# Two-layer block with 16 routed experts on one core: the last batch's scatter, the second half's plan and its pads move among the routed tiles, with eight result buffers

## The chip, the core and the metric

The kernel runs on one core of a Trainium2 chip. The core has TensorE (PE: matmuls and transposes), VectorE (DVE), ScalarE (ACT) and GpSimd (POOL); SyncE (SP) only issues transfers. Transfers with addresses that are computed on the chip (indirect DMAs) are issued by POOL here, all others by SP. The metric is the device time of one execution, in microseconds.

## The reference

Input are 32 sequences of 512 tokens with 256 features, in float32. First comes an attention layer with 16 heads in 4 groups, causal and with rotary positions, between two layer norms and with a residual. Then comes a layer of experts, and the cut below is this one. The kernel computes only the two experts of each token that the router chose.

```python
def _L0_ffn_ref(x, gate_w, gate_b, shared_wg, shared_wu, shared_wd, experts_wg, experts_wu, experts_wd):
    E, TOP_K = 16, 2
    router_logits = jax.nn.sigmoid(x @ gate_w + gate_b)
    expert_values, expert_indices = jax.lax.top_k(router_logits, k=TOP_K)
    expert_values = expert_values / jnp.sum(expert_values, axis=-1, keepdims=True)
    ...
    expert_weighted = jnp.sum(expert_values[..., None] * selected, axis=2)
    return x + _mlp(x, shared_wg, shared_wu, shared_wd) + expert_weighted
x = x + _layernorm(_L0_attn_ref(_layernorm(x)))
x = x + _layernorm(_L0_ffn_ref(_layernorm(x)))
```

(`selected` are the outputs silu(x wg) * (x wu) times wd, 128 wide inside, of the chosen experts.)

## The kernel before

There are two programs for each engine, one after the other, in two blocks, and every engine waits for every other between them.

**The first block** (`attention_phase`) takes the 32 batches through attention, the norms and the router, several batches at once in an order written out by hand. For each batch b DVE ends with the slots (L1094): the place of each token in the list of each of its two experts. POOL then writes the batch's 512 rows to those places in `sorted_dram`, in eight indirect DMAs (`scatter`, L658: four groups of 128 tokens, two experts each), which wait for `slots_ready` and for the copy of the rows, `h2_copied`. The batches are in two halves of 16, each with lists of its own. After the last batch of a half DVE plans its tiles: 28 small steps in three lumps, `plan_ends`, `plan_tiles` and `plan_limits` (L1104 to L1148), which turn the counts of the experts into a table: for each tile its expert, its first row and the limit behind which its rows are padding. SP stores this table (`plan_dram`, L527, elements of 4 bytes, 3 KB in all). Each expert's last tile is filled up with 128 rows of padding, one indirect DMA (a pad) for each of the 16 experts: those of the first half are issued inside attention, and those of the second, whose lists get the last rows only at the very end, inside the second block.

**The boundary** (L330) is a barrier: each engine drains, which includes the transfers that POOL has issued, and then they go on together.

**The second block** (`expert_phases`) begins with SP loading both plans (L1297, L1298) and then the rows of the tiles. Each half has at most 143 tiles of 128 rows, and 286 tiles are run in a fixed order. In turn t:

- SP loads the 128 rows of tile t into one of `RD` = 8 buffers (L1313), as soon as the result of tile t - 8 is taken (`y_taken`, `named`).
- PE transposes the hidden values of tile t - 2 (L1448), the rows of tile t + 1 (L1428), multiplies the rows of tile t by the gate and up weights (L1440, signals `hidden`) and the hidden values of t - 2 by the down weights (L1454).
- ACT copies the transposed hidden values of t - 2 (L1537), takes the silu of tile t (L1531, one instruction to a tile) and halves the rows of t - 2 (L1543).
- DVE copies the transposed rows of t + 1 (L1593), multiplies gate and up of tile t (L1600), works out where the results of t - 2 go (L1609, L1612) and forms the results (L1621) in one of `YD` = 4 buffers. Both of the latter wait until the store of the tile that used the buffer before has landed (`y_stored`).
- POOL waits for `named` and `y_taken`, does one tiny instruction on a cell (L199) and issues the indirect store of the results (L1367). Up to tile 15 it issues one pad of the second half behind it (L1372).

At turn 1, DVE also turns the limits of both halves into two tables, `keep` and `aside` (L1632, L1635, L1639, over 512 columns). When the loads of tile 143 on are issued, SP waits for all scatters and pads of the second half. After the tiles comes the shared expert with the last norm, over 32 batches, to the end.

## Time and profile before

| | us |
|---|---|
| median of three runs | 2648.06 (2647.75 to 2649.0) |
| profiled execution, its time | 2651.59 |
| profiled execution, its span | 2649.8 |
| attention, to the last matmul before the boundary | about 1878 |
| boundary: PE without work | 30.71, up to 1909.17 |
| routed tiles | 1909 to about 2440 |
| shared expert and last norm | 2440 to 2650 |

Over the span PE is busy for 2402.8 us (91%), DVE for 1980.9 (75%), ACT for 1503.2 (57%) and POOL for 1636.4 (62%). The mean granted clock of TensorE is 0.964 of full speed, and it is lower in three places, the start, the boundary and the first tiles. These shares are means over stages with different limits, and so the rows further down are taken from the boundary and the tiles alone. The span runs from the first instruction to the last; the execution's time is 1.8 us more.

### The profile page before, as it was taken

The page shows a single profiled execution, that of the slowest core. Times are in us where ns is not written, and L with a number is a line of the kernel's source. Part 1 is how long each engine was busy: PE and PEld are TensorE (multiplying, and loading weights), DVE is VectorE, ACT ScalarE, POOL GpSimd, SP SyncE. Part 2 cuts the span into 40 slices and gives each one's busy share as a digit, 9 for nine tenths or more (in the row PEclk, how much of TensorE's full clock was granted, in tenths as well). Part 3 has the DMA queues.
Part 4 walks back from the last instruction along what each step waited for, and adds up shares of the span by engine and source line. Part 5 has one row for each costly group of instructions (what it writes and reads, how often), then busy time and mean ns, then how long its engine had stood idle before and what let it go on. Part 6 is the DMA issues. An engine that isn't in the chain of part 4 may idle for free. (4 is left out here: it accounts for less than half of the span.)

```text
span 2649.8 us, 60700 instructions
## 1 busy us (share of the span) xinstructions
PE 2402.8 (91%) x18798; PEld 1582.8 (60%) x18798; DVE 1980.9 (75%) x5220; ACT 1503.2 (57%) x3420; POOL 1636.4 (62%) x2761
## 2 busy tenths in 40 slices
PE   4999999999999999898999999998279999999997
PEld 2565556655566555555655566554168777877664
DVE  5677878778787788677778787874347777776887
ACT  1566666666666666565566666665124444444554
POOL 2446665666656666665666656653266666666886
PEclk7899999999999999999999999999579999999998
DMA  4354445544455443444434444332346546544996
GB/s 124 93 151 123 136 127 153 151 123 135 128 153 151 122 135 121 121 143 144 138 118 123 121 146 146 110 103 74 65 139 190 151 147 200 159 145 156 304 349 237
DMA packets 288652, 388.00 MB, mean 146 GB/s; under 512 B 27922, under 2 KB 238098, under 8 KB 288212
## 3 DMA queue, kind: packets, MB, share of 16 engines
q1 hardware_dynamic: 260788, 308.56, 39.6%
q0 software_dynamic: 27552, 75.57, 8.3%
q8 instruction: 161, 2.64, 0.4%
q14 instruction: 151, 1.24, 0.2%
HBM read 193.40 MB, written 172.27 MB: 138 GB/s over the span
## 5 line engine op out<-in xcount | busy, mean ns | idle before, releaser
L847 ACT ACTIVATE probs<-ps_a 128x512 f32<-128x512 f32 (+1 forms) x1408 | 727.8, 561 | 463.3 <-PE ps_a L731 386.6
L967 DVE TENSOR_REDUCE negmax<-ps_d 128x2 f32<-128x768 f32 (+3 forms) x768 | 788.3, 1040 | 264.2 <-PE ps_d L715 219.8
L713 PE MATMUL ps_d<-ks,qs 96*128 96x128 bf16 (+3 forms) x2048 | 489.2, 305 | 83.5 <-DVE negmax L967 61.7
L729 PE MATMUL ps_a<-qs,ks 99*128 99x512 bf16 (+3 forms) x2048 | 515.0, 305 | 22.3 <-DMA qs<-k_parts_negmax_t 10.2
L731 PE MATMUL ps_a<-mask_exp,ident_bf 128*128 128x128 bf16 x2048 | 396.9, 221 | 0.0
L715 PE MATMUL ps_d<-mask_max,ident_bf 128*128 128x128 bf16 x2048 | 394.9, 222 | 0.0
L1367 POOL DMA_INDIRECT y_dram<-ysb,to_row x286 | 282.3, 987 | 118.5 <-issue 82.3
L713 PEld LDWEIGHTS ps_d<-ks,qs 96*128 96x128 bf16 x2048 | 202.7, 99 | 239.9 <-issue 80.2
L743 PE MATMUL ps_out<-probs,va 128*32 128x512 f32 (+3 forms) x4096 | 333.6, 444 | 0.0
L199 POOL TENSOR_TENSOR pool_cell<-zero_col 1x1 f32<-1x1 f32 x318 | 58.7, 185 | 437.0 <-DVE slot L1094 375.1
L729 PEld LDWEIGHTS ps_a<-qs,ks 99*128 99x128 bf16 x2048 | 201.1, 99 | 187.7 <-issue 39.3
L1440 PE MATMUL ps_gu<-wgu,rows_t 128*128 x1144 | 303.5, 389 | 6.7 <-DVE rows_t L1593 5.3
L658 POOL DMA_INDIRECT sorted_dram<-h,slot x256 | 255.1, 997 | 66.0 <-issue 65.2
L1531 ACT ACTIVATE gate<-ps_gu 128x128 f32<-128x128 f32 x286 | 79.6, 278 | 266.3 <-issue 137.6
L731 PEld LDWEIGHTS ps_a<-mask_exp,ident_bf 128*128 128x128 bf16 x2048 | 203.1, 99 | 29.1 <-issue 19.9
L1440 PEld LDWEIGHTS ps_gu<-wgu,rows_t 128*128 128x128 f32 x1144 | 200.5, 196 | 25.4 <-issue 9.0
L1454 PE MATMUL ps_y<-wd,hid_t 128*128 x572 | 182.7, 402 | 23.4 <-ACT hid_t L1537 22.9
L715 PEld LDWEIGHTS ps_d<-mask_max,ident_bf 128*128 128x128 bf16 x2048 | 203.0, 99 | 0.7 <-issue 0.7
L743 PEld LDWEIGHTS ps_out<-probs,va 128*32 128x32 f32 x4096 | 108.2, 110 | 141.8 <-issue 105.0
L1600 DVE TENSOR_TENSOR hid<-ps_gu,gate 128x128 f32<-128x128 f32 x286 | 83.3, 291 | 120.2 <-ACT gate L1531 96.4
L1593 DVE COPY rows_t<-ps_t 128x256 f32<-128x256 f32 x286 | 118.9, 416 | 35.6 <-PE ps_t L1428 35.1
L1621 DVE SCALAR_TENSOR_TENSOR ysb<-ps_y,rows,half_row 128x256 f32<-128x256 f32 x286 | 138.4, 484 | 9.1 <-PE ps_y L1454 4.2
(200 smaller groups left out, 4516.7 us busy)
## 6 DMA issues: line engine op xcount, KB each, us to landing
qs<-q_stack_dram SPq DMA_DIRECT2D x128, 384.0 KB, 5.8
rows<-sorted_dram SPq DMA_DIRECT2D x286, 129.0 KB
y_in<-y_dram SPq DMA_DIRECT2D x32, 1024.0 KB
q_stack_dram<-q_parts SPq DMA_DIRECT2D x64, 384.0 KB
x_in<-in_x SPq DMA_DIRECT2D x32, 512.0 KB
q_stack_dram<-q_parts SPq DMA_DIRECT2D x64, 256.0 KB
x<-in_x SPq DMA_DIRECT2D x32, 512.0 KB
h_dram<-h SPq DMA_DIRECT2D x32, 512.0 KB, 3.0
```

The lines of the kernel that those rows point to most:

```text
L658: pool.indirect_dma_start(out=sorted_dram[b // (B // 2)][:, :], in_=h2[:, k, j, :], in_offset=None, out_offset=bass.IndirectOffsetOnAxis(a ...
L713: pe.matmul(ps_d[:, number % 2, at:at + width], qs[0:KR, b % 2, h, j * P:(j + 1) * P], ks[0:KR, b % 2, g, 0:width], start=True, stop=False)
L715: ins = pe.matmul(ps_d[:, number % 2, at + j * P:at + (j + 1) * P], ident_bf[:, :], mask_max[:, :], start=False, stop=True)
L729: pe.matmul(ps_a[:, number % 3, at:at + width], ks[0:KM, b % 2, g, j * P:(j + 1) * P], qs[0:KM, b % 2, g * HG + h0 + k, j * P:T], start=Tr ...
L731: ins = pe.matmul(ps_a[:, number % 3, at:at + P], ident_bf[:, :], mask_exp[:, :], start=False, stop=True)
L743: ins = pe.matmul(ps_out[32 * h:32 * h + 32, j * P:T], va[:, b % 3, j, g * 32:(g + 1) * 32], probs[:, at:at + width], start=(j == 0), stop ...
L847: act.activation(probs[:, at:at + nh * width], ps_a[:, number % 3, 0:nh * width], ACT.Exp) \
L967: dve.tensor_reduce(negmax[:, g // 2, j, at:at + nh], src, AX_X, ALU.max, negate=True) \
L1367: pool.indirect_dma_start(out=y_dram[:, :], in_=ysb[:, k, :], in_offset=None, out_offset=bass.IndirectOffsetOnAxis(ap=to_row[k][:, 0:1].bi ...
L1440: ins = pe.matmul(ps_gu[:, t % 2, 0:2 * I], rows_t[:, t % 2, c, :], wgu[:, expert[t], c, :], start=(c == 0), stop=(c == NC - 1))
L1454: pe.matmul(ps_y[:, t % 2, 0:D], hid_t[:, t % 2, :], wd[:, expert[t], :], start=True, stop=True) \
L1621: dve.scalar_tensor_tensor(out=ysb[:, k, :], in0=ps_y[:, t % 2, 0:D], scalar=rows[:, t % RD, D + 1:D + 2], in1=half_row[:, t % 2, :], op0= ...
```

## The change

It has four parts, all around the boundary.

1. The eight scatters of the last batch (b = 31) are no longer issued in the first block. POOL issues them in the second, one behind the result store of each of the tiles 1, 4, 7, ... 22 (`scatter_last`).
2. The plan of the second half leaves the first block as well. DVE does its lumps behind tiles 30, 36 and 42 (`PLAN_AT` = 30); SP stores the table behind the load of tile 46 and loads it back behind that of tile 54. At the start SP loads the first half's plan alone. `keep` and `aside` are formed for each half by itself, at turns 1 and 70.
3. The 16 pads of the second half, issued behind tiles 0 to 15 before, are issued behind tiles 54, 57, ... 99 (`PADS_AT` = 54).
4. There are eight buffers of tile results (`YD` = 8) in place of four.

The buffers that both blocks now use are declared outside of both, and the planning steps stand in a class, `Plan`; the steps themselves are as before. New waits: DVE waits for `plan_stored` before the second plan and for `limits_loaded` at turn 70; SP for `planned` behind tile 46, `plan_stored` behind tile 54, and `plan_loaded` behind tile 142; PE for `plan_loaded` at tile 143.

```diff
-RD, YD = 8, 4
+RD, YD = 8, 8
...
-                if c == B // 2 + 1 or c == B + 1:
-                    half = c // B
-                    sp.wait_ge(planned, half + 1)
-                    sp.dma_start(plan_dram[half].rearrange("w (q p) -> p w q", p=P), tile_plan_i[:, :, :],
+                if c == B // 2 + 1:
+                    sp.wait_ge(planned, 1)
+                    sp.dma_start(plan_dram[0].rearrange("w (q p) -> p w q", p=P), tile_plan_i[:, :, :],
...
-                    if exists(c - 2):
+                    if exists(c - 2) and c - 2 < B - 1:
...
-                        if c - 2 in (B // 2 - 1, B - 1):
+                        if c - 2 == B // 2 - 1:
                             if at == SIDE["plan_ends"]:
-                                plan_ends((c - 2) // (B // 2))
+                                plan.ends(0)
...
+            def load_plan(half):
+                sp.wait_ge(v["plan_stored"], 16 * (half + 1))
+                sp.dma_start(plan_row[:, half, :, :], plan_dram[half, 0:2, :].unsqueeze(0)).then_inc(plan_loaded, 16)
+                sp.dma_start(limits[:, half, :], plan_dram[half, 2, :].bitcast(F32).partition_broadcast(P)) \
+                    .then_inc(limits_loaded, 16)
+
+            load_plan(0)
...
                 load_rows(t)
+                if t == PLAN_AT + 16:
+                    sp.wait_ge(v["planned"], 2)
+                    sp.dma_start(plan_dram[1].rearrange("w (q p) -> p w q", p=P), v["tile_plan_i"][:, :, :],
+                                 allow_slow_non_contiguous=True) \
+                        .then_inc(v["plan_stored"], 16)
+                if t == PLAN_AT + 24:
+                    load_plan(1)
+                if t == TILES - 1:
+                    sp.wait_ge(plan_loaded, 16 * 2)
...
+            def scatter_last(i):
+                if i == 0:
+                    pool.wait_ge(v["slots_ready"], B)
+                    pool.wait_ge(v["h2_copied"], 16 * B)
+                j, k = i // 2, i % 2
+                pool.indirect_dma_start(
+                    out=sorted_dram[1][:, :], in_=v["h2"][:, k, j, :], in_offset=None,
+                    out_offset=bass.IndirectOffsetOnAxis(ap=v["slot"][(B - 1) % 2][:, j, k:k + 1], axis=0),
+                ).then_inc(v["scattered"][(B - 1) % 2], 16)
+
+            def pad_last(e):
+                if e == 0:
+                    pool.wait_ge(v["planned"], 2)
+                pool.indirect_dma_start(
+                    out=sorted_dram[1][:, :], in_=v["pad_row"], in_offset=None,
+                    out_offset=bass.IndirectOffsetOnAxis(ap=v["pad_at"][:, 1, e:e + 1], axis=0),
+                ).then_inc(v["padded"], 16)
...
-                if t < E:
-                    pool.indirect_dma_start(
-                        out=sorted_dram[1][:, :], in_=v["pad_row"], in_offset=None,
-                        out_offset=bass.IndirectOffsetOnAxis(ap=v["pad_at"][:, 1, t:t + 1], axis=0),
-                    ).then_inc(v["padded"], 16)
+                if t % 3 == 1 and t // 3 < 2 * NT:
+                    scatter_last(t // 3)
+                if t >= PADS_AT and (t - PADS_AT) % 3 == 0 and (t - PADS_AT) // 3 < E:
+                    pad_last((t - PADS_AT) // 3)
...
                 if t == 1:
-                    dve.wait_ge(limits_loaded, 16)
...
+                    pads_aside(0)
+                if t == PLAN_AT:
+                    plan.ends(1)
+                if t == PLAN_AT + 6:
+                    plan.tiles(1)
+                if t == PLAN_AT + 12:
+                    plan.limits(1)
+                if t == PLAN_AT + 40:
+                    pads_aside(1)
```

In the programs of the engines it shows at these places. In the rows, `x8` is a run of eight alike, and what stands in brackets are the semaphores waited for.

POOL at the boundary and behind it, before (L658 are the scatters of batch 31, L330 is the boundary, L1353 the start of the second block):

```order
L641 TENSOR_SCALAR shift<-guess 128x4 [waits root_steps]
L199 TENSOR_TENSOR pool_cell<-zero_col 1x1 [waits h2_copied,paused,slots_ready,ln_ready2]
L658 DMA sorted_dram<-h,slot 133248x258 x8
L330 UNCONDITIONAL_BRANCH
L1353 UNCONDITIONAL_BRANCH [waits barrier_Pool_Activation_PE_DVE_SP_gather]
L1356 IOTA own_row 128x512
```

All eight scatters stand here ahead of the boundary, and they leave this place. POOL at the same place, now (L386 is the boundary, L1409 the result store of a tile, L1391 a scatter of batch 31):

```order
L703 TENSOR_SCALAR shift<-guess 128x4 [waits root_steps]
L386 UNCONDITIONAL_BRANCH [waits ln_ready2]
L1377 UNCONDITIONAL_BRANCH [waits barrier_Pool_Activation_PE_DVE_SP_gather]
L1380 IOTA own_row 128x512
L1382 MEMSET eps 128x4
L1383 MEMSET minus_half 128x4
L199 TENSOR_TENSOR pool_cell<-zero_col 1x1 [waits y_taken,named,numbered]
L1409 DMA y_dram<-ysb,to_row 69376x256
L199 TENSOR_TENSOR pool_cell<-zero_col 1x1 [waits paused2,y_taken,named]
L1409 DMA y_dram<-ysb,to_row 69376x256
L1391 DMA sorted_dram<-h,slot 133248x258 [waits h2_copied,slots_ready]
L199 TENSOR_TENSOR pool_cell<-zero_col 1x1 [waits paused2,y_taken,named]
```

The eight scatters have left the front of the boundary, and the first of them stands behind the second tile's result store.

POOL in the first tiles, before (L1372 is a pad):

```order
L199 TENSOR_TENSOR pool_cell<-zero_col 1x1 [waits y_taken,named,numbered]
L1367 DMA y_dram<-ysb,to_row 69376x256
L1372 DMA sorted_dram<-wgu,pad_at 133248x258
L199 TENSOR_TENSOR pool_cell<-zero_col 1x1 [waits paused2,y_taken,named]
L1367 DMA y_dram<-ysb,to_row 69376x256
L1372 DMA sorted_dram<-wgu,pad_at 133248x258
L199 TENSOR_TENSOR pool_cell<-zero_col 1x1 [waits paused2,y_taken,named]
```

There was one pad to each tile here; there is now one scatter to every third tile, and the pads stand in the same way, one to every third, from tile 54 on.

SP around the store of the second plan, now (L1328 is a load of rows, L1324 the reading of a tile's first row from the plan):

```order
L1328 DMA rows<-sorted_dram 128x258
L1324 TENSOR_LOAD plan_row
L1324 ISA x2
L1328 ISA [waits named,y_taken]
L1328 DMA rows<-sorted_dram 128x258
L1354 DMA plan_dram<-tile_plan_i 128x6x1 [waits planned]
L1324 TENSOR_LOAD plan_row
L1324 ISA x2
```

The store stands between two loads of rows; before, it was SP's last instruction ahead of the boundary.

## Rows read from the trace of the kernel before

**Rows 1.** Windows of all engines: us, busy and instructions by engine, TensorE clock, DMA share, GB/s.

```profile
1881.00:1904.00 23.00, 0.00 (x0) 0.00 (x0) 4.79 (x28) 0.00 (x0) 8.02 (x9) 0.50 0.44 46
...
1912.00:1974.00 62.00, 44.83 (x176) 35.35 (x175) 26.86 (x97) 15.15 (x57) 35.56 (x52) 0.78 0.42 128
1974.00:2036.00 62.00, 61.16 (x329) 50.63 (x328) 46.17 (x180) 29.65 (x110) 42.13 (x72) 1.00 0.64 192
```

**Rows 2.** Block boundary line L330: engine op xcount: ns min/median/max, first and last start.

```profile
L330 POOLq DRAIN  x1: 19010/19010/19010, 1884.8 to 1884.8; - x1
L330 DVEq DRAIN  x1: 268/268/268, 1886.4 to 1886.4; - x1
```

**Rows 3.** Timeline at the boundary: start, us, engine line op out<-in [idle before <-releaser].

```profile
1881.01 0.20 POOL L199 TENSOR_TENSOR pool_cell<-zero_col 1x1 f32<-1x1 f32 x1 [13.77 <-DVE slot L1094]
...
1881.69 1.09 POOL L658 DMA_INDIRECT sorted_dram<-h,slot  x1 [0.48 <-issue]
...
1886.61 0.36 SPq L527 DMA_DIRECT2D plan_dram<-tile_plan_i  x1
...
1890.68 0.96 POOL L658 DMA_INDIRECT sorted_dram<-h,slot  x1 [0.30 <-issue]
1904.05 0.64 SPq L1297 DMA_DIRECT2D plan_row<-plan_dram  x1
...
1909.17 0.66 PE L1428 MATMUL ps_t<-ident,rows 128*128 128x128 f32 x2 [30.71 <-DMA rows<-sorted_dram]
```

**Rows 4.** Windows of line L1531, one ACT gate for each tile (x is tiles).

```profile
1912.00:1974.00 62.00, 5.59 (x20) 0.78 0.42 128
1974.00:2036.00 62.00, 10.21 (x37) 1.00 0.64 192
```

**Rows 5.** Timeline of POOL in the stretch with a pad at every tile.

```profile
1949.93 0.99 POOL L1367 DMA_INDIRECT y_dram<-ysb,to_row  x1 [0.15 <-issue]
1951.22 0.96 POOL L1372 DMA_INDIRECT sorted_dram<-wgu,pad_at  x1 [0.30 <-issue]
...
1955.75 0.99 POOL L1367 DMA_INDIRECT y_dram<-ysb,to_row  x1 [0.47 <-issue]
```

**Rows 6.** Timeline of ACT at the end of that burst.

```profile
1953.66 0.28 ACT L1531 ACTIVATE gate<-ps_gu 128x128 f32<-128x128 f32 x1 [5.26 <-PE ps_gu L1440]
```

**Rows 7.** Timeline of POOL later, with result stores alone.

```profile
2020.17 0.99 POOL L1367 DMA_INDIRECT y_dram<-ysb,to_row  x1 [0.42 <-issue]
...
2022.18 0.99 POOL L1367 DMA_INDIRECT y_dram<-ysb,to_row  x1 [0.76 <-POOL pool_cell L199]
...
2023.54 0.99 POOL L1367 DMA_INDIRECT y_dram<-ysb,to_row  x1 [0.16 <-issue]
```

**Rows 8.** Timeline of ACT in the same stretch, gates alone.

```profile
2023.05 0.28 ACT L1531 ACTIVATE gate<-ps_gu 128x128 f32<-128x128 f32 x1 [0.82 <-PE ps_gu L1440]
...
2028.89 0.28 ACT L1531 ACTIVATE gate<-ps_gu 128x128 f32<-128x128 f32 x1 [0.82 <-PE ps_gu L1440]
```

**Rows 9.** Windows of PE among the pads: us, PE busy, TensorE clock, DMA share, GB/s.

```profile
1929.00:1933.00 4.00, 3.23 (x9) 0.50 0.21 67
```

**Rows 10.** Waits of DVE from 1904 to 2440: us in total, times, longest.

```profile
DVE kept_row L1609 <- DMA y_dram<-ysb,to_row: 4.4, 5, 1.4
```

**Rows 11.** Timeline of DVE at the third tile.

```profile
1914.46 0.48 DVE L1632 TENSOR_SCALAR keep<-limits,row_no 128x512 int32<-128x512 f32 x1
...
1915.49 0.69 DVE L1639 TENSOR_TENSOR aside<-limits,own_row 128x512 int32<-128x512 f32 x1
```

**Rows 12.** Windows of all engines around both plan stores (L527 at 1067.66 and 1886.61).

```profile
1062.00:1067.00 5.00, 5.00 (x55) 3.18 (x44) 3.06 (x9) 4.65 (x11) 2.39 (x3) 1.00 0.81 252
...
1069.00:1074.00 5.00, 4.94 (x51) 4.33 (x49) 4.81 (x15) 3.07 (x7) 0.65 (x1) 1.00 0.62 36
1074.00:1079.00 5.00, 4.53 (x33) 2.33 (x30) 1.72 (x9) 1.06 (x2) 3.90 (x6) 1.00 0.38 47
```

**Rows 13.** Line L713 from 1075 to 1090: what PE sat idle for before it.

```profile
  DVE negmax L967: 7.0, 1
```

More of the change, by code:

```diff
@@ L298, in layer @@
         counts = sb("counts", [P, NT + 1, E])
+        h2 = sb("h2", [P, 2, NT, ROW])
+        slot = [sb(f"slot{k}", [P, NT, 2], U32) for k in range(2)]
+        tile_ends, tiles_of, jumps, spare = (sb(n, [P, E]) for n in ("tile_ends", "tiles_of", "jumps", "spare"))
+        tiles_i = sb("tiles_i", [P, E], I32)
+        past, jumped = sb("past", [P, TQ, E]), sb("jumped", [P, TQ, E])
+        tile_plan = sb("tile_plan", [P, 3, TQ])
+        tile_plan_i = sb("tile_plan_i", [P, 3, TQ], I32)
         pool_cell, dve_cell = sb("pool_cell", [1, 2]), sb("dve_cell", [1, 2])
@@ L317, in attention_phase @@
         v[n] for n in ("q_stack_dram", "k_stack_dram", "h2_dram", "sorted_dram", "plan_dram"))
[L318 to L321 removed]
+    wgu, wd, ident, h2, slot, tile_plan_i = (v[n] for n in ("wgu", "wd", "ident", "h2", "slot", "tile_plan_i"))
+    slots_ready, h2_copied, planned = (v[n] for n in ("slots_ready", "h2_copied", "planned"))
     (h2_std, h2_mean, counts, pool_cell, dve_cell, zero_col, tile_no, row_no) = (
@@ L338, in sem @@
             return ctx.enter_context(nc.semaphore(name))
+        wq = sb("wq", [P, NC, 2, P])
+        wkv = sb("wkv", [P, NC, P])
+        bq = sb("bq", [P, 2])
+        bk = sb("bk", [P, 1])
+        rope = sb("rope", [P, 4, T])
+        wo = sb("wo", [P, NC, D])
+        bo = sb("bo", [P, D])
+        gate_w = sb("gate_w", [P, NC, 2 * E])
+        act_bias = sb("act_bias", [P, NC + 2])
+        ident_bf = sb("ident_bf", [P, P], BF16)
+        mask_max = sb("mask_max", [P, P], BF16)
+        mask_exp = sb("mask_exp", [P, P], BF16)
+        before = sb("before", [P, P], BF16)
+        ones_bf = sb("ones_bf", [P, P], BF16)
+        iota_e = sb("iota_e", [P, E])
+        token = sb("token", [P, NT])
         x_in = sb("x_in", [P, 2, NT, D])
@@ L1140, in plan_limits @@
-            def plan_limits(half):
-                do(dve.tensor_tensor(jumps[:, 0:E - 1], spare[:, 1:E], spare[:, 0:E - 1], ALU.subtract))
-                do(dve.tensor_tensor(jumped[:, :, 0:E - 1], past[:, :, 0:E - 1],
-                                     jumps[:, 0:E - 1].unsqueeze(1).to_broadcast([P, TQ, E - 1]), ALU.mult))
-                do(dve.tensor_reduce(tile_plan[:, 2, :], jumped[:, :, 0:E - 1], AX_X, ALU.add))
-                do(dve.scalar_tensor_tensor(out=tile_plan[:, 2, :], in0=tile_no[:, :, 0], scalar=-float(P),
-                                            in1=tile_plan[:, 2, :], op0=ALU.mult, op1=ALU.add))
-                dve.tensor_scalar(tile_plan_i[:, 2, :].bitcast(F32), tile_plan[:, 2, :], spare[:, 0:1], None, ALU.add) \
-                    .then_inc(planned, 1)
-                plan.end()
+            plan = Plan(dve, v)
@@ L1155, in _ @@
                     if step == "side":
-                        if c - 2 in (B // 2 - 1, B - 1):
+                        if c - 2 == B // 2 - 1:
                             if at == SIDE["plan_ends"]:
-                                plan_ends((c - 2) // (B // 2))
+                                plan.ends(0)
                             if at == SIDE["plan_tiles"]:
-                                plan_tiles((c - 2) // (B // 2))
+                                plan.tiles(0)
                             if at == SIDE["plan_limits"]:
-                                plan_limits((c - 2) // (B // 2))
+                                plan.limits(0)
                         if exists(c - 1):
@@ L1206, in _ @@
                             first_split(2)
+PLAN_AT, PADS_AT = 30, 54
 PLAN_STEPS = 3 + 8 + 3 + 10 + 4
@@ L1622, in take_y, with pads_aside @@
                                          in1=half_row[:, t % 2, :], op0=ALU.mult, op1=ALU.add).then_inc(y_taken, 1)
+            plan = Plan(dve, v)
+            def pads_aside(half):
+                dve.wait_ge(limits_loaded, 16 * (half + 1))
+                dve.tensor_scalar(keep[:, half, :], limits[:, half, :], row_no[:, 0:1], -1.0, ALU.is_gt, ALU.mult) \
+                    .then_inc(kept, 1)
+                dve.wait_ge(kept, 3 * half + 1)
+                dve.tensor_scalar(limits[:, half, :], limits[:, half, :], row_no[:, 0:1], None, ALU.is_le) \
+                    .then_inc(kept, 1)
+                dve.wait_ge(kept, 3 * half + 2)
+                if half == 0:
+                    dve.wait_ge(numbered, 3)
+                dve.tensor_tensor(aside[:, half, :], limits[:, half, :], own_row[:, half, :], ALU.mult) \
+                    .then_inc(kept, 1)
+                dve.wait_ge(kept, 3 * half + 3)
             take_turned(0)
```

135 lines of the change are left out of this document (56 added, 79 removed).

## The prediction, made before the changed kernel had run

> **What bounds the kernel now.** I read the windows first, from the end of attention on. Three stretches differ. Between 1881 and 1904 PE and ACT do nothing at all, DVE runs 28 instructions and POOL nine [rows 1]: that is the boundary between the two blocks. From 1912 to 1974 PE is busy 44.8 of 62.0 us at a mean granted clock of 0.78, from 1974 on it is busy 61.2 of 62.0 at 1.00 [rows 1]. So the tiles are bounded by PE once they run, and by something else in their first 62 us. The gates, one to a tile, size it: 20 tiles in the first 62 us, 37 in the next [rows 4]. A steady tile takes 62/37 = 1.68 us, 20 of them 33.5 us, so the first stretch has an **excess of 28.5 us**.
>
> Next, what ends the boundary. POOL's drain takes 19.01 us from 1884.8, to 1903.8; DVE's takes 0.27 from 1886.4 [rows 2]. Ahead of it stand the eight scatters of batch 31, which start at 1881.69, as soon as DVE has the slots, and are issued by 1891.6; then nothing is issued until 1904.05, and PE's first transpose is at 1909.17 [rows 3]. The boundary waits for the eight scatters to be done, not for the plan.
>
> Last, what fills the first stretch. POOL issues a result store and a pad for each tile, 1.29 us apart, and after such a burst stands still for 4.5 us (1951.22 to 1955.75) [rows 5]. ACT waits 5.26 us for PE's gate product until 1953.66, 1.5 us after the burst's last instruction [rows 6], and PE's clock falls to 0.50 in 1929 to 1933 [rows 9]. The trace doesn't say why PE's result is taken so late. It shows that this comes with POOL's back-to-back transfers, and in small without pads: stores at 2020.17, 2022.18 and 2023.54, one 0.4 us late and the next catching up at 1.36 [rows 7], and then three gate intervals of 5.84 us in all, 2023.05 to 2028.89 [rows 8], against 5.03 for three steady tiles.
>
> **The change, part by part.** The sum is made against the profiled span of 2649.8 us. That run took 2651.6, 3.5 above the median of 2648.1, so 3.5 comes off at the end.
>
> Boundary. Without scatters and plan, POOL, DVE and SP have nothing after the slots, which were there at 1881.0 [rows 3]. POOL's branch then comes at about 1881.2 in place of 1903.8: **-22.6**. What is late next is the plan's load, which doesn't move against the barrier. This term needs batch 30's scatters to be drained by then: POOL had been idle for 13.77 us before 1881.01 [rows 3], more than the 12.2 that the drain lasted after the last scatter (1891.6 to 1903.8), so I leave nothing of it out.
>
> Sixteen pads away from tiles 0 to 15. The excess is 28.5 us. Something remains of it: the first tiles start at half clock, and the three wide steps of the third tile run from 1914.46 to 1916.18 [rows 11], now over half the width. I leave 3 for both: **-25.5**.
>
> 24 extra transfers among tiles, eight scatters behind tiles 1 to 22 and 16 pads behind tiles 54 to 99, one to every third tile. Bounds. Below: POOL needs 1.36 + 1.36 + 1.29 + about 1.3 = 5.3 us for three tiles with one extra [rows 5, 7], PE gives 5.03, so POOL falls 0.3 us behind by each, 2.4 us over the scatters and 4.8 over the pads; eight buffers (8 x 1.68 = 13.4 us of tiles) hold that, and the extras cost 0. Above: 28.5/16 = 1.78 each, 43. The nearest row is the small catch-up without pads: 5.84 - 5.03 = 0.8 for one short interval [rows 8]. With an extra POOL has two short intervals, not one, and the backlog isn't paid back before the next extra. I take 1.0 each: **+24**. A buffer more doesn't help there, since what is late is PE's product and not a buffer: DVE waited for a stored result only 5 times, 4.4 us in all [rows 10].
>
> DVE steps among tiles. The 28 steps fill 4.79 us busy [rows 1], some 5.8 with their gaps, in three lumps of about 2.3, 2.3 and 1.2 behind tiles 30, 36 and 42, and three steps over 256 columns behind tile 70 (0.9 us). DVE is busy 46.2 of 62.0 us over 37 tiles [rows 1], 0.43 us free in each, so a lump delays multiply, and PE with it, by about its length less 0.43: 1.9 + 1.9 + 0.8 + 0.4, less 0.9 for the halved steps at tile 1: **+4**, between 1 and 6.
>
> Second plan store among tiles. It is a transfer of four-byte pieces. The first one, issued at 1067.66 amid attention, is followed by 10 us in which the core moves 36 and 47 GB/s where it had moved 252 [rows 12], and PE then stands 7.0 us for DVE [rows 13]. In the old place the second one froze nobody, as all waited for the drain. Now it stands on SP behind the load of tile 46. SP loads rows eight buffers ahead, but each load waits until the result eight tiles back is taken, two tiles behind its gates, so rows have 5 tiles (8 us) at most between issue and use, less 2 us to land. A freeze of 10 leaves 4 or more. **+5**, between 0 (the tile traffic gets through) and 12 (7 plus a stretch at the low clock). SP's own waits for plan and load hold only row loads, far ahead.
>
> The Trainium skill, page "DMA: Bandwidth & Descriptors", section Specifications, says that transfers below 512 bytes are done as read-modify-write and miss line rate. That speaks against this change: the only such store moves from an idle stretch into a busy one. It agrees with the low rates in [rows 12]; by it alone, since the 3 KB are few, the store would cost its own queue and not the others, and the sum would be 5 us lower.
>
> Eight buffers. They can remove the 4.4 us of waits [rows 10], partly hidden behind PE: **-2**, between 0 and 4.4. The tail, 2440 to the end, isn't touched: 0.
>
> Sum: -22.6 - 25.5 + 24 + 4 + 5 - 2 = **-17.1**, a span of 2632.7, a run of 2634.5 and a median of **2631.0**. With every bound at its best (0 for the extras, -28.5 for the pads, 1, 0, -4.4) it is -54.5, 2594; at its worst (43, 6, 12, 0) +12.9, 2661.
>
> **Rivals.** *The eight buffers hide the extras.* For it: POOL's backlog of 0.3 us for each extra is far under eight tiles, and the stalls of the first stretch came in step with four tiles, the old number of buffers (eight POOL instructions, a pause, eight more). Against it: DVE's few waits for a stored result. The extras then cost 2 or so, the sum is -39, the median 2609.
>
> *Full price.* Each extra costs what a pad cost, 1.78, as every one makes two transfers follow at once and what is late doesn't depend on spacing. +43 in place of +24: +1.6 in all, median 2650, no change.
>
> *Slower: POOL is never idle and PE falls to its low clock again and again.* Place: tiles 1 to 30 and 54 to 120, where POOL works off the backlog at 0.3 us a tile. In the first stretch a cycle was four tiles in about 13.7 us where 6.7 would do, 7 us lost, half of it by the clock (0.50 in [rows 9]). From the seventh such cycle on (49 us in place of 24) the kernel is over 0.2% slower with the other terms as above: the sum is +8 with seven, +22 with nine; in the middle, +15, a median of 2663. Against it: between extras POOL gets two tiles to breathe, and a short lag doesn't let the clock fall (1.00 in 1974 to 2036 with such lags in it).
>
> *The boundary doesn't shrink* (something else drains until about 1892): 11 us come back, 2642. POOL's 13.77 idle us speak against it.
>
> **How the numbers follow.** Forecast, extras near 1 us each: 0.48. Buffers hide them: 0.24. Full price: 0.12. Slower: 0.11. Boundary shrinks by half: 0.05. A measurement of this kernel can tell about 0.2% (5.3 us) from no change, so "same" is 2642.8 to 2653.4. Faster: 0.46 of the forecast, 0.24, and 0.03 of the boundary: 0.73. Same: 0.02, 0.11, 0.02: 0.15. Slower: 0.01 of full price, 0.11: 0.12. Range: 2598 to 2654 leaves out the slow case and the extreme of the hidden one, together under 0.2.
>
> **What would show it.** In the changed profile: the drain of POOL short and the first transpose at about 1886.5; gates in the first 62 us of tiles about 33 in place of 20; around tiles 54 to 99 three gates in 6.0 us (5.0 if the buffers hide the pads, 6.8 at full price); a stop of rows after the plan store behind tile 46, with PE idle about 5 us; POOL's 1.3 us intervals not followed by an ACT wait of 5 us. Wrong would be the forecast if PE's clock stays below 0.9 in tiles 1 to 22 (the slow case), or if the steady stretch after tile 100 has other than 37 gates in 62 us, as then the buffers or their traffic change the steady state, which no term above holds.

## The result, and the profile after

The changed kernel took 2654.4 us (median of 20 runs, 2647.6 to 2658.7) beside 2645.9 for the kernel before (20 runs, 2641.4 to 2655.6): a ratio of **1.0029, 95% interval 1.0021 to 1.0037**. It is slower by 8.5 us, where 17 us less were forecast (a median of 2631.0, between 2598 and 2654). The profiled execution has a span of 2653.2 us against 2649.8.

The time of either kernel depends on the chip it runs on. In six measurements there were two kinds of chip: on the slower kind, which this first measurement belongs to by its times, the kernel before takes 50 to 60 us longer and the changed kernel 92 to 96 us longer. The section on experiments shows both.

**The boundary went as forecast.** Line L386 is the boundary now, its columns are those of [rows 2]:

```profile
L386 POOLq EVENT_SEMAPHORE  x2: 17/17/17, 1877.1 to 1877.2; - x2
L386 POOLq COMPARE_BRANCH  x1: 38/38/38, 1863.4 to 1863.4; - x1
L386 POOLq DRAIN  x1: 7907/7907/7907, 1863.6 to 1863.6; - x1
...
L386 DVEq DRAIN  x1: 205/205/205, 1876.8 to 1876.8; - x1
```

POOL is drained at 1871.5 already (batch 30's scatters), and DVE, whose drain starts when the slots of batch 31 are there, is last. The first gate of the tiles is at 1885.4, in place of 1912.7: 27.3 us earlier.

**The tiles gave it back.** Windows of the gates (L1574, one for each tile), to be held against [rows 4]:

```profile
core 0: us, ACT busy (x), PEclk, DMA share, GB/s
1885.00:1947.00 62.00, 7.53 (x27) 0.97 0.48 144
1947.00:2009.00 62.00, 7.77 (x28) 0.94 0.60 156
2009.00:2071.00 62.00, 7.26 (x26) 0.94 0.45 132
2071.00:2133.00 62.00, 7.24 (x26) 0.92 0.44 127
2133.00:2195.00 62.00, 9.72 (x35) 1.00 0.50 149
```

Four windows have 26 to 28 tiles, where the kernel before has 37 in an undisturbed one. The clock is the lesser part of the loss: its mean is 0.92 to 0.97 in these windows, and 0.92 stands for 10 of the 62 us at the lower level, 5 us of work at most (an estimate) of the 20 that the window loses. In the run with spread steps (third group) the window 2071 to 2133 has 28 tiles at a clock of 1.00. The table adds up the distances of the gates and takes 1.625 us off for each tile, the median distance in the traces of the quicker chips; what is left is called the excess, in us. (The prediction took 1.68 us for a steady tile, which makes 1.1 us in 20 tiles.)

| tiles | what stands there now | before | after | moved by | forecast |
|---|---|---|---|---|---|
| 0 to 30 | 8 scatters (before: 16 pads) | 30.0 | 18.9 | -11.1 | -17.5 |
| 30 to 50 | plan steps, plan store | 1.1 | 15.2 | +14.1 | +9 |
| 50 to 110 | 16 pads | 7.4 | 39.8 | +32.4 | +16 |
| 110 to 285 | nothing | 20.3 | 16.9 | -3.4 | -2 |
| first gate | the boundary | | | -27.3 | -22.6 |

With the last phase (215.2 us from the last gate to the end before, 213.8 after) the sum is +3.3, the difference of the spans.

**What an extra transfer does.** The pads' stretch, POOL first (start, us, engine, line), then ACT at the same time:

```profile
2013.94 0.98 POOL L1409 DMA_INDIRECT y_dram<-ysb,to_row  x1 [0.46 <-issue]
2015.23 0.96 POOL L1399 DMA_INDIRECT sorted_dram<-wgu,pad_at  x1 [0.31 <-issue]
...
2016.55 0.98 POOL L1409 DMA_INDIRECT y_dram<-ysb,to_row  x1 [0.16 <-POOL pool_cell L199]
...
2017.91 0.98 POOL L1409 DMA_INDIRECT y_dram<-ysb,to_row  x1 [0.16 <-issue]
...
2020.97 0.98 POOL L1409 DMA_INDIRECT y_dram<-ysb,to_row  x1 [0.46 <-issue]
```

```profile
2015.00 0.28 ACT L1574 ACTIVATE gate<-ps_gu 128x128 f32<-128x128 f32 x1 [0.82 <-PE ps_gu L1483]
...
2018.23 0.28 ACT L1574 ACTIVATE gate<-ps_gu 128x128 f32<-128x128 f32 x1 [2.42 <-PE ps_gu L1483]
...
2019.91 0.28 ACT L1574 ACTIVATE gate<-ps_gu 128x128 f32<-128x128 f32 x1
...
2022.08 0.28 ACT L1574 ACTIVATE gate<-ps_gu 128x128 f32<-128x128 f32 x1 [0.82 <-PE ps_gu L1483]
```

One pad makes three short intervals in a row (1.29, 1.32, 1.36 us): the pad itself, and two result stores that catch up. In that time ACT waits 2.42 us for a gate product whose last matmul ends at 2016.59; the gate starts 1.64 us after that end, where the gates around it start at once, and ACT takes the transposes behind it 2.6 us late. Then 3.06 us pass from the last store's start to the next one's. From one first store to the next, 2013.94 to 2020.97, are 7.03 us for three tiles; undisturbed they take 4.88. **This extra costs 2.15 us.** 15 of the 24 extras show the three short intervals (7 of 24 in the second trace of this kernel on such a chip); in the others one or two follow, or five and more before a pause of some 4.2 us. The means over all extras, further down, are about 2 us.

What it does to PE is seen in its waits over all the tiles, here and on a quicker chip (second group), where the extras are the same:

```profile
PE ps_y L1497 <- ACT hid_t L1580: 41.7, 32, 2.1
```

```profile
PE ps_y L1497 <- ACT hid_t L1580: 0.9, 2, 0.4
```

The first line is from 1877 to 2443, the second from 1851 to 2351 there (us in total, times, longest). PE waits 41.7 us, in 32 waits, for hidden values that ACT copies late, against 0.9 us in 2.

**The plan store.** Windows of all engines around it (issued at 1979.87), as in [rows 12], and PE's waits from 1975 to 2000:

```profile
1975.00:1980.00 5.00, 5.00 (x29) 4.29 (x29) 3.66 (x18) 2.05 (x9) 3.13 (x5) 1.00 0.37 112
1980.00:1985.00 5.00, 4.29 (x21) 2.75 (x19) 4.02 (x17) 2.17 (x9) 3.24 (x6) 1.00 0.89 34
1985.00:1990.00 5.00, 0.00 (x0) 0.00 (x0) 0.29 (x1) 0.22 (x1) 1.42 (x3) 0.80 0.69 56
1990.00:1995.00 5.00, 3.90 (x12) 3.20 (x13) 1.43 (x6) 0.85 (x3) 0.00 (x0) 0.52 0.83 277
```

```profile
PE ps_t L1469 <- DMA rows<-sorted_dram: 6.4, 1, 6.4
```

As in attention, 10 us at 34 and 56 GB/s follow the store; PE waits 6.4 us for rows, and comes back at a granted clock near the lower level (0.52). The store holds up POOL's queue as well as SP's own: it moved 48 packets from 1975 to 1978, and 2 from 1981 to 1984, though two result stores were issued in that time. (A load of 512 KB that SP issues at 1983.39, behind tile 48 in both kernels, stands in the same stop; in the kernel before, without the store, tiles 30 to 50 have an excess of 1.1 us with it.)

### The profile page after: what moved, and what is told of

Read it like the earlier page. It is cut to its first block and busy times, and to the rows that moved or that the text cites. A ratio compares the mean times of both kernels' runs of the same rounds, so it can differ in the third digit from the quotient of the medians.

```text
span 2653.2 us, 60704 instructions
## 1 busy us (share of the span) xinstructions
PE 2402.5 (91%) x18798; PEld 1577.5 (59%) x18798; DVE 1979.4 (75%) x5223; ACT 1501.4 (57%) x3420; POOL 1631.5 (61%) x2760
## 5 line engine op out<-in xcount | busy, mean ns | idle before, releaser
L791 PE MATMUL ps_a<-qs,ks 99*128 99x512 bf16 (+3 forms) x2048 | 513.2, 304 | 23.2 <-DMA qs<-k_parts_negmax_t 11.1
L1409 POOL DMA_INDIRECT y_dram<-ysb,to_row x286 | 281.6, 985 | 111.4 <-issue 78.7
L720 POOL DMA_INDIRECT sorted_dram<-h,slot x248 | 246.8, 995 | 63.5 <-issue 62.6
L1574 ACT ACTIVATE gate<-ps_gu 128x128 f32<-128x128 f32 x286 | 79.4, 278 | 278.3 <-PE ps_gu L1483 151.6
L1497 PE MATMUL ps_y<-wd,hid_t 128*128 x572 | 183.5, 403 | 42.8 <-ACT hid_t L1580 41.7
L1483 PEld LDWEIGHTS ps_gu<-wgu,rows_t 128*128 128x128 f32 x1144 | 199.8, 195 | 27.7 <-issue 11.4
L1497 PEld LDWEIGHTS ps_y<-wd,hid_t 128*128 128x128 f32 x572 | 96.0, 193 | 91.9 <-issue 76.8
```

The source lines that it names most:

```text
L720: pool.indirect_dma_start(out=sorted_dram[b // (B // 2)][:, :], in_=h2[:, k, j, :], in_offset=None, out_offset=bass.IndirectOffsetOnAxis(a ...
L791: pe.matmul(ps_a[:, number % 3, at:at + width], ks[0:KM, b % 2, g, j * P:(j + 1) * P], qs[0:KM, b % 2, g * HG + h0 + k, j * P:T], start=Tr ...
L1409: pool.indirect_dma_start(out=y_dram[:, :], in_=ysb[:, k, :], in_offset=None, out_offset=bass.IndirectOffsetOnAxis(ap=to_row[k][:, 0:1].bi ...
L1483: ins = pe.matmul(ps_gu[:, t % 2, 0:2 * I], rows_t[:, t % 2, c, :], wgu[:, expert[t], c, :], start=(c == 0), stop=(c == NC - 1))
L1497: pe.matmul(ps_y[:, t % 2, 0:D], hid_t[:, t % 2, :], wd[:, expert[t], :], start=True, stop=True) \
```

## The experiments

The kernel before ran beside every group and tells the chip's kind. It took 2590.6, 2590.6 and 2589.9 us on three chips, and 2649.6 and 2639.6 on two; the first measurement (2645.9, on a chip that isn't recorded) is like the second kind. Below these are **quick chips** and **late chips**, after what their traces show. Each chip was measured in one group only, so no run shows whether the kind belongs to the chip for good, or to something else that lasted for the group. "Excess" is counted from the gates as in the table above, in the profiled execution of each kernel.

### First group, on a quick chip (kernel before 2590.6)

**Pads issued by SP.** POOL's `pad_last` is gone, and SP has behind the same tiles (cut; ahead of tile 143 it waits for `sp_padded`)

```diff
+ pad_to = sp.value_load(v["pad_at"][0:1, 1, e:e + 1].bitcast(I32), min_val=0, max_val=LIST - P)
+ sp.dma_start(sorted_dram[1][bass.ds(pad_to, P), :], v["pad_row"]).then_inc(sp_padded, 16)
```

> The changed kernel, with the 16 pads issued by SP as ordinary transfers at a row read from the plan, in place of POOL's indirect ones, behind the same tiles (54, 57, ... 99). The bytes and the place are the same, the engine and the way of issue differ. Theory A (what costs is an indirect transfer more on POOL, which makes PE's signals arrive late; from the changed kernel's trace about 2.2 us each): tiles 50 to 110 lose their excess, the time falls by 16 x 2.2 = 35 us to about 2619. Rival B (the extra traffic itself, or its writes to sorted_dram, holds up the loads of rows): no change, 2650 to 2658.

**Scatters back ahead of the boundary** (`scatter_last` is gone, the condition `c - 2 < B - 1` too):

> The changed kernel, with the last batch's eight scatters put back ahead of the boundary; plan, pads and eight buffers stay as changed. Theory A: the first 30 tiles lose the scatters' price (about 16 us of their 19 us excess), and the boundary gets the drain of eight indirect transfers back, 22 us if it lasts as before, some 12 if the plan store, which is no longer there, had lengthened it: a time of 2650 to 2661. If scatters among tiles were cheap (my forecast of 1 us each, 8 in all), it would be 2658 to 2669.

**Second plan back ahead of the boundary**, steps and store:

> The changed kernel, with the second half's plan and its store back ahead of the boundary; scatters and pads stay among the tiles, both still spaced by three. In the changed kernel's trace tiles 30 to 50 have an excess of 15 us, 9 of it at the plan store. If steps and store cause it: -14 in these tiles, and +6 for the 28 steps before the boundary, and 0 to +10 since the store now slows the first loads behind the boundary: 2646 to 2656, with the gates of tiles 30 to 50 at 1.63 to 1.68 us. If the scatters' backlog caused it, these tiles stay slow and the time is 2660 or more.

**Four result buffers** (`YD = 4`):

> The changed kernel with four result buffers in place of eight. Theory A (PE's signals are late, buffers play no part): 0 to +6, 2654 to 2660. Rival C (eight buffers do hide part of the extras): +15 or more. Rival D (eight buffers let POOL fall further behind and make the delays longer): below 2648.

| | time | ratio to before | first gate | excess 0-30 | 30-50 | 50-110 |
|---|---|---|---|---|---|---|
| pads by SP | 2561.2 | 0.9896 (0.9868 to 0.9923) | 1856.3 | 1.2 | 14.9 | 4.2 |
| scatters back | 2580.8 | 0.9973 (0.9962 to 0.9985) | 1872.8 | 1.2 | 16.0 | 2.7 |
| plan back | 2560.8 | 0.9886 (0.9866 to 0.9905) | 1872.1 | 1.0 | 0.9 | 2.3 |
| four buffers | 2572.8 | 0.9939 (0.9915 to 0.9963) | 1856.0 | 2.0 | 15.7 | 6.6 |

None of my expected times came, as the kernel before itself was 55 us quicker than in the first measurement. The table still says much. In all four kernels the scatters or pads that stand among the tiles cost next to nothing. With them on SP or on POOL the time is the same (2561.2 here, 2562.3 in the next group), which taken alone spoke against Theory A (its text is above: an indirect transfer more on POOL makes PE's signals late) and for no price at all; the third group shows on which chips it holds. The scatters ahead of the boundary cost 16.5 us of first gate and 19.6 us of time against the first row; without the plan store POOL's drain there takes 15.4 us, not 19. The plan costs 15 us in tiles 30 to 50 or as much ahead of them (first gate 15.8 later: the engines pass the boundary at 1857.3 in place of 1848.1, some 6 of that for the steps and the rest since the slots came later, and the first gate then comes 14.8 us behind it in place of 8.2): it is worth the same in either place. Four buffers were slower than the first and third row by 11 to 12 us, though its ratio's interval still overlaps the first row's a little, so on this kind of chip the buffers do seem to pay.

### Second group, again on a quick chip (2590.6)

> The kernel before, unchanged, as a run of its own with a trace. In the first round of experiments the kernel before took 2590.6 us, not the 2646 to 2648 measured earlier, and no trace of that round shows PE's signals late. If that is a property of the chip it ran on (theory P), a trace of the kernel before from such a chip shows no late gates: pads at every tile cost only POOL's own time (16 x (2.62 - 1.63) = 16 us at most for the first 16 tiles, less what four buffers hide), in place of 28.5, and no hiccups later. Rival Q: the kernel before still has late signals there, and the gain came from attention alone.

> The changed kernel, unchanged, beside the kernel before on the same chip. Theory P: where the signals are not late, the 24 extras cost nothing, and the change is worth the boundary (-27), the pads (-10 to -16), less the plan store and the steps (+15): ratio 0.990 to 0.993. On a chip with late signals: 1.003 as first measured. If eight buffers are what costs (rival D), the ratio is above 1 on either chip, while the version with four buffers was at 0.994.

> The kernel before with eight result buffers and nothing else. Theory P without late signals: with a pad at every tile POOL needs 2.62 us a tile against 1.63; eight buffers let PE run on for about 8 tiles (backlog 8 us) and no further, four for about 4: 4 to 6 us gained, ratio 0.998. With late signals buffers play no part: ratio 0.999 to 1.001. If eight buffers cost something by themselves: above 1.002.

> The changed kernel with the eight scatters in one burst at POOL's start in the second block, ahead of the first result store, in place of one to every third tile. The burst takes 8 x 1.3 = 10 us and ends when tile 3 or so is through. Without late signals: the same as the changed kernel within 3 us. With late signals: one delay of 4 to 8 us in place of 16 over the first 24 tiles, so 8 to 12 us less than the changed kernel.

| | time | ratio to before | first gate | excess 0-30 | 30-50 | 50-110 |
|---|---|---|---|---|---|---|
| kernel before | 2589.4 | 0.9998 (0.9986 to 1.0011) | 1885.4 | 15.2 | 0.7 | 1.9 |
| changed kernel | 2562.3 | 0.9890 (0.9865 to 0.9915) | 1859.2 | 0.4 | 16.6 | 2.0 |
| before, eight buffers | 2580.2 | 0.9965 (0.9946 to 0.9984) | 1876.1 | 7.7 | 1.2 | 1.7 |
| changed, scatters in a burst | 2566.1 | 0.9903 (0.9878 to 0.9928) | 1863.6 | 1.8 | 16.2 | 2.5 |

**On a quick chip the same change makes the kernel 1.1% faster.** Here is why, in the pads' stretch of the changed kernel there, POOL and then ACT:

```profile
1988.31 0.99 POOL L1409 DMA_INDIRECT y_dram<-ysb,to_row  x1 [0.16 <-POOL pool_cell L199]
...
1989.66 1.00 POOL L1409 DMA_INDIRECT y_dram<-ysb,to_row  x1 [0.16 <-POOL pool_cell L199]
...
1991.02 0.99 POOL L1409 DMA_INDIRECT y_dram<-ysb,to_row  x1 [0.16 <-POOL pool_cell L199]
1992.31 0.96 POOL L1399 DMA_INDIRECT sorted_dram<-wgu,pad_at  x1 [0.30 <-issue]
```

```profile
1988.85 0.28 ACT L1574 ACTIVATE gate<-ps_gu 128x128 f32<-128x128 f32 x1 [0.82 <-PE ps_gu L1483]
...
1990.47 0.28 ACT L1574 ACTIVATE gate<-ps_gu 128x128 f32<-128x128 f32 x1 [0.82 <-PE ps_gu L1483]
...
1992.10 0.28 ACT L1574 ACTIVATE gate<-ps_gu 128x128 f32<-128x128 f32 x1 [0.82 <-PE ps_gu L1483]
```

POOL issues the same transfers at the same 1.29 to 1.36 us, here without a pause, and the gates come every 1.62 us all the same. (The next one, at 1994.65, is 0.9 us late, but there PE itself starts 0.67 us late, for DVE, which has just done the three steps behind tile 70.) Over the pads' tiles 50 to 110, the gates that start more than 0.3 us after the last recorded matmul of a gate product are 18 in the first trace and 20 in its repetition on a late chip, and none in any trace from a quick chip. So back-to-back indirect transfers don't make PE's signals late by themselves; they do on some chips. The kernel before shows it too: its gates are 29, 37 and 38 to a window on a quick chip, and 20 and 37 in [rows 4]. What is left of its first excess, 15.2 us in tiles 0 to 30, is POOL's own pace of 2.62 us a tile with a pad, and eight buffers take half of it. Of the 60.9 us between its two spans, 27.3 lie before the first gate (1912.7 and 1885.4) and 32.2 in the tiles.

The same change is worth more here than was forecast, by another sum. The spans differ by 27.0 us: -26.2 at the first gate, -14.8 in tiles 0 to 30, +15.9 in tiles 30 to 50, nothing in 50 to 110, and -2 behind them.

The burst costs 3.8 us against the changed kernel by the medians, about the 3 that were allowed. Eight buffers in the kernel before are worth 9 us by the ratio (4 to 14 by its interval), more than the 4 to 6 expected; the profiled execution, 9 us quicker than their median, has 7.5 us less in tiles 0 to 30.

### Third group, on a late chip (kernel before 2649.6)

The store cut in six, `[:, i // TQ, i % TQ:i % TQ + 1]` behind each of six loads, and the plan's methods turned into generators, of which DVE takes one step a tile from tile 14 on:

> The changed kernel once more, for whatever chip this round has. The kernel before tells the condition: about 2590 without late signals of PE, about 2646 with them. Theory P: 0.989 in the first, 1.003 in the second.

> The changed kernel with the second plan's store cut into six of 128 elements, one behind each of the loads of tiles 46 to 51. In the changed kernel the one store is followed by a stop of the loads of 8 to 9 us (tiles 44 to 47). If the row loads queue behind the store's 768 small pieces, a sixth of it (some 1.5 us) hides in the 3 us by which rows are early: 8 us less than the changed kernel. If it is a fixed cost of any such store, six cost more than one: slower than the changed kernel.

> The changed kernel with the second plan's DVE steps one to a tile, behind tiles 14 to 38, in place of three lumps behind tiles 30, 36 and 42. Where one step of 0.2 us fits into DVE's 0.4 us free in each tile, the 6 us excess of tiles 30 to 40 goes: 5 to 6 us less than the changed kernel. If each step costs a wait of its own, nothing is gained.

> The changed kernel with three edits: the store in six pieces, the steps one to a tile, and the 16 pads issued by SP in place of POOL. Without late signals the pads cost nothing anyway, and the sum is -8 and -6: about 2548, ratio 0.984. With late signals the pads' 35 us come off too: 2605 against 2646.

| | time | ratio to before | excess 0-30 | 30-50 | 50-110 |
|---|---|---|---|---|---|
| changed kernel | 2658.1 | 1.0026 (1.0011 to 1.0040) | 21.0 | 15.2 | 40.4 |
| store in six | 2659.7 | 1.0033 (1.0017 to 1.0049) | 19.0 | 18.5 | 38.5 |
| steps spread | 2650.5 | 1.0009 (1.0000 to 1.0019) | 18.8 | 9.6 | 35.6 |
| both, pads by SP | 2624.6 | 0.9908 (0.9878 to 0.9938) | 20.8 | 11.7 | 8.0 |

The first result repeats on a chip of the late kind. The pads are the test: same bytes, same places, but issued by SP, and their stretch falls from 40.4 to 8.0, which is **2.0 us for each pad** and Theory A of the first group. That run has the two other edits too, but each of them alone leaves the stretch at 38.5 and 35.6; and the next group has a run that differs from "steps spread" in the pads' issue alone, on another late chip, with 5.1 there, or 1.9 us for each pad. With the pads by SP no gate of that stretch is late by the count of the second group. The gates of that stretch (L1611 there) are back at 35 and 37 to a window, against 26 and 26:

```profile
2009.00:2071.00 62.00, 9.72 (x35) 0.97 0.64 186
2071.00:2133.00 62.00, 10.28 (x37) 1.00 0.56 165
```

Spreading the steps takes 5.6 us out of tiles 30 to 50 (7.7 by the medians), as expected. Cutting the store in six does not help: 3 us more are lost in these tiles, though the times can't be told apart (2658.1 and 2659.7). From a load's issue to DVE's copy of its transposed rows are 12 to 14 us for the loads in its midst, 11 to 12 behind the single store, and 6 undisturbed. Six stores don't cost six times one, so the price is hardly that of a transfer; that it goes by the 768 elements is likely and not tested by a store of another size.

### Fourth group, on a late chip (2639.6)

> The kernel before with one edit: the 16 pads of the second half are issued by SP as ordinary transfers, one behind each of the first 16 loads, in place of POOL's. With late signals (the kernel before at about 2648): the excess of the first 20 tiles falls from 29 to 3 or so, 2622, ratio 0.990. Without (about 2590): 12 to 15 us, since POOL's own 2.6 us a tile bounded the first 20 to 30 tiles there: 2577, ratio 0.995. If the bytes of the pads and not their issue held up the tiles: 1.000.

> The changed kernel with the pads issued by SP and the DVE steps of the plan one to a tile; the plan store in one piece again. Against the version with six pieces: 1 to 3 us less. With late signals 2620, ratio 0.989; without 2556, ratio 0.987.

> The version with pads on SP and spread steps, with four result buffers in place of eight. If buffers play no part in the price of the scatters: within 3 us of the eight-buffer version, with the same excess of tiles 0 to 30 (about 20 us with late signals, 1 without). If eight buffers pay: 5 us or more slower. If eight buffers prolong the delays: 5 us or more faster, with late signals alone.

> The version with pads on SP and spread steps, with the eight scatters in one burst ahead of the first result store. With late signals: if the price is one for each time that POOL falls behind (theory), one delay of 4 to 8 us in place of the 16 over 24 tiles, 8 to 12 us less than the spaced version; if it is a price for each transfer: no difference. Without late signals: 2 to 4 us slower than the spaced version, as the burst is in the way of the first stores.

| | time | ratio to before | first gate | excess 0-30 | 30-50 | 50-110 |
|---|---|---|---|---|---|---|
| before, pads by SP | 2621.5 | 0.9933 (0.9912 to 0.9953) | 1909.8 | 11.4 | 0.7 | 3.9 |
| pads by SP, steps spread | 2609.2 | 0.9893 (0.9870 to 0.9915) | 1879.9 | 21.5 | 11.8 | 5.1 |
| the same, four buffers | 2611.4 | 0.9910 (0.9885 to 0.9936) | 1877.0 | 17.6 | 9.8 | 6.8 |
| the same, scatters in a burst | 2594.9 | **0.9845 (0.9821 to 0.9869)** | 1875.7 | 3.1 | 9.3 | 6.1 |

In the kernel before, pads by SP take the first 30 tiles from an excess of 30.0 (in the first trace, [rows 4]) to 11.4, in place of the 3 expected; the time of 2621.5 is the expected one, but the kernel before was 8 us quicker on this chip than the 2648 that the expectation started from, and the gain is 18 us and not 26. The trace shows what is left: SP takes 1.1 us for a load and 1.1 for a pad (loads start at 1905.21, 1907.43 and 1909.65, a pad between each two), so with a pad at every tile it hands out rows every 2.2 us where a tile takes 1.63, and from 1919.77 on the gates follow at 2.2 to 2.6 us. Sixteen tiles at 0.6 us too many make some 9 of the 11.4 us, an estimate from these times. SP has room for a pad at every third tile, not at every one. Four and eight buffers are the same within the intervals on a late chip, and the price of the scatters is there with both, so the buffers don't cause it. The burst wins 14 us. Its POOL (L1423 is a scatter there) and the next result store (L1444):

```profile
1867.64 1.09 POOL L1423 DMA_INDIRECT sorted_dram<-h,slot  x1 [0.29 <-POOL minus_half L1415]
...
1876.63 0.96 POOL L1423 DMA_INDIRECT sorted_dram<-h,slot  x1 [0.30 <-issue]
1880.73 0.18 POOL L199 TENSOR_TENSOR pool_cell<-zero_col 1x1 f32<-1x1 f32 x1 [3.13 <-DVE ysb L1695]
1881.38 0.99 POOL L1444 DMA_INDIRECT y_dram<-ysb,to_row  x1 [0.47 <-POOL pool_cell L199]
```

Four start before PE has its first rows (first transpose at 1871.65), seven before the first gate (1875.7), and POOL then waits 3.13 us for the first result. My reason for this run, one delay for each burst, is not what it shows: the burst meets hardly any signals of PE that could be late. The first gate starts as its product ends, and the next two are 0.4 and 0.7 us late. Excess 3.1 against 21.5 also prices the spaced scatters: **2.3 us each**. The best version on a late chip is this one, and it beats both kernels there. (3.1 and 21.5 are of one profiled execution each; the medians, 14.2 us apart, make it 1.8 us each.)

### Fifth group, on a quick chip (2589.9)

The first kernel replaces PE's `value_load` of the expert by `t % TILES * E // TILES`, so it leaves out the right choice of the weights, and that part of its result is wrong; the second puts the pads back on POOL, eight behind tile 54 and eight behind tile 86.

> The changed kernel without PE's reading of the tile's expert from the plan: the expert is a number fixed by the tile's place, so the rows meet the wrong weights and that part of the result is left wrong; everything else, the extras too, stays. If the register load on PE is what is held up behind POOL's traffic, and the signals behind it (theory R): with late signals the 2.2 us for each extra go, 2658 becomes about 2610. If the signals themselves are held up (theory S): within 5 us of the changed kernel, with the same excess of 18 to 20 us in tiles 0 to 30 and 40 in tiles 50 to 110. Without late signals (kernel before at 2590) it tells nothing: 2560 either way.

> The version with spread steps and the scatters in one burst, with the pads on POOL again, in two bursts of eight behind tiles 54 and 86. POOL falls 10 us behind by each, 6 tiles of eight buffers. With late signals, if each burst costs one delay (about as long as POOL is busy without a pause, 10 to 20 us, less what PE does meanwhile): excess of tiles 50 to 110 of 15 to 30, against 8 with pads on SP and 40 with spaced pads. If a price for each transfer: 35 to 40. Without late signals: 0 to 3.

They took 2558.2 us (0.9876, 0.9848 to 0.9904) and 2562.3 us (0.9891, 0.9865 to 0.9917). As said beforehand, a quick chip can't tell the theories of either apart. Both questions stay open: what holds PE's signals on a late chip, and what a burst amid the tiles costs there. The second run shows that, on a quick chip, eight buffers take two bursts of eight with 5.5 us of excess in tiles 50 to 110.

## Why the prediction was wrong, point by point

- **Boundary, -22.6: right**, -27.3 in this pair and -26.2 on the quick chip. POOL's drain was the wait, and it went. Some 4 and 2 us of it is that the slots themselves came earlier in these executions.
- **Early pads, -25.5: right** in size on a late chip: with the scatters out of the way too (the burst), tiles 0 to 30 keep 3.1 us.
- **24 extras, +24 at 1.0 each: the step that failed.** They cost about 2 us each on a late chip (1.8 to 2.3 by the runs above): about 16 in tiles 0 to 30 where 8 were booked, 32 in tiles 50 to 110 where 16 were. I took the price from one catch-up with one short interval, [rows 8], and wrote in the same place that an extra makes two; the trace shows three in a row. By [rows 8] a short interval costs 0.8 to 1.0 us and by the three here 0.7, so the price should have been a multiple of that row, not the row. (That it goes by the number of short intervals is my reading; no run varies that alone.) A sign that I had listed shows it: 6.0 us for three gates around the pads, and 6.8 at full price; three stores take 7.0. My upper bound of 1.78, from pads at every tile, was no bound either: there the delays of one burst of eight were shared by four pads; spaced by three tiles, most extras start a delay of their own. So spacing did not make an extra cheaper, about 2 us against 1.78; whether it makes it dearer is not shown, as the run that was to compare the two on a late chip met a quick one.
- **Rival "the buffers hide them"** is what happens on a quick chip (excess 2.0 for 16 pads, and 6.6 with four buffers), where PE's signals are not late. On a late one it is wrong. **Rival "full price"** came nearest in its sum (2650). **Rival "slower"** had the sign, but not the mechanism: it wanted half of each loss from the clock, and the clock stayed at 0.92 and above in these windows, a quarter of their loss at most.
- **DVE steps, +4: right**, up to 5.6 by the run that spreads them, within the bounds of 1 to 6.
- **Plan store, +5: right in kind and too small**, some 9: what is left of tiles 30 to 50 when the steps are spread is 9.6, and 1 of it was there before. The 7 us of [rows 13] were the better row than my 4 to 5 by slack, since the clock's fall comes on top. The Trainium skill, page "DMA: Bandwidth & Descriptors", section Specifications, states that transfers below 512 bytes are done as read-modify-write and don't reach line rate. The low rates here agree (34 and 56 GB/s); that its own queue alone would pay, as I had put it from there, doesn't: the loads of 129 KB behind it stand still, and so do POOL's result stores (2 packets in 3 us after 48).
- **Eight buffers, -2: not contradicted** on the late chip (2.3 us by time, which is within the intervals and so can't be told from nothing); some 10 us on a quick one. The steady stretch is as it was: 35 to 38 gates to a window behind 2133, and 3.4 us less excess.

Sum as measured: -27.3 - 11.1 + 14.1 + 32.4 - 3.4 - 1.4 = +3.3. With the extras at 1.0 it would have been about -21. On a quick chip the forecast has the right sign for the wrong reasons, and that is luck: the 24 us for extras that cost nothing there stand against 11 us too many for the early pads (15 in place of 25.5) and 7 too few for the plan.

## What to carry to other kernels

Work moved off a barrier onto an engine "with room" is priced by what that engine's busy stretches do to the others, and the row to take is one with as many short intervals in a row as the new pattern makes. Contiguous blocks at a computed row don't need POOL's indirect transfer: SP with a register for the row did the same work, and its stretch was back at the kernel before's excess (8.0 and 7.4 us), as long as SP itself has the 1.1 us to spare. On a late chip, transfers that no one waits for belonged where the engines stand still anyway, in a burst, and not spread thinly over a full pipeline (14 us); on a quick chip the burst was 4 us slower. And a verdict of 1% on one chip can turn its sign on another.

## What the runs showed of the hardware

- Chips differ in a way that turns the sign of a change: the kernel before took 2590 us on three chips and 2640 to 2650 on two, and the changed one stood at 0.989 on one of the first kind and at 1.003 in two measurements of the second. On the second kind PE's results are taken late while POOL issues indirect transfers back to back: the gate of [rows 6], at 1953.66 after a wait of 5.26 us, stands 4.5 us behind the end of its product's last matmul (1949.17). On the first kind the same pace leaves ACT's wait at 0.82 us. What differs is not known.
- A store of 3 KB in 4-byte elements holds up the core's other transfers for some 10 us (34 and 56 GB/s), and six stores of 128 elements do so no less.
- Eight indirect transfers ahead of a barrier are issued in 10 us. POOL's drain behind them took 19.0 and 19.6 us with the plan store in its midst, and 15.4 us without.
- SP takes 1.1 us to issue a transfer at a row that it reads from a table.
